# Gated cross-attention block: scores as stacked 96-row contractions, projections one section earlier, mask as pairs of 64-row matmuls

## The chip, the cores and the metric

One core of one Trainium2 chip runs the whole kernel. The metric is the device time of one execution in microseconds (us), as the median of several runs. The profile shows one further execution, with its own time.

## The reference

The input x has 128 sequences of 128 tokens of width 256; ctx has the same shape. Per sequence:

```python
x = x + tanh(g_xattn) * mha(layernorm(x), ctx, ctx)   # 16 heads of 16, causal, biases on q, k, v, o
x = x + tanh(g_ffn) * bitlinear(silu(bitlinear(n, w_gate)) * bitlinear(n, w_up), w_down)   # n = layernorm(x)
```

The attention is softmax(q k / 4) v with a causal mask. A bitlinear rounds each activation row to 8 bits by the row's maximum and the weight matrix to three values by its mean magnitude; the inner width is 1024. All inputs and outputs are float32.

## The kernel before

A tile is one sequence: 128 tokens on the partitions. Two sequences are a pair, and there are 64 pairs. Setup loads and transposes the weights, splits the attention weights into a high and a low part (F32R), rounds the feed-forward weights, and fills constants. The main part is written out in full by Python loops: a section belongs to one tile, `s` is 0 for even tiles and 1 for odd ones, and each engine's `body(c)` lists its work in a section. Every engine runs its list in order, and semaphores connect the engines.

The work is staged. In the section of tile t the kernel does the attention of tile t, the output projection of t-1, the gate and up matmuls of t-2 and the down projection of t-3, and it projects for the next pair: K in an even section (`s` = 0), Q and V in an odd one. Products of F32R operands take three terms, high x high, low x high and high x low (`TERMS`).

The scores of a half (eight heads, two PSUM banks, S_B[half]) are six matmuls of 512 columns (L507). The keys stand in `k_blk` block-diagonally for four heads at a time: 64 rows hold the four heads, and the other 64 rows hold pieces of the causal mask, with matching selection rows in `q_t`. SP makes `k_blk` by eight DMAs a pair out of `k_t` (L473), in the odd section. Q's high part is cast on ACT (`q_high`, L757), its low part made on DVE (`q_low`, L935).

After the scores, DVE takes the row maxima (`top`, L849). For half 0 DVE subtracts the maximum into `prob` (`shift`, L856) and ACT takes exp of it (L711). For half 1 ACT takes exp with the maximum as its bias in eight instructions (L717). PE transposes the probabilities (L515), ACT copies them to `prob_t` (L724), and PE multiplies them with the values (L526); a column of ones gives the row sums. ACT copies the result to `o_raw`, PE transposes it back (L533), DVE divides (L862, L865), PE transposes again (L539), ACT and DVE split it (L736, L880), and PE projects it (L549). PE's wait list for that is

```python
pe.wait_ge(ot_hi, c.tile(1))
pe.wait_ge(ot_lo, c.tile(1))
wait(pe, y_ok, c.tile(3))
```

where `y_ok` counts the results y (`result`, L944): the down projection and the output projection share a bank. Then DVE adds the residual (`residual`, L888), takes the norm's statistics (L891, L895), and POOL centres and rounds the rows.

The feed-forward has gate and up matmuls per half (L607) into one bank each, tanh on ACT (L732), and two instructions per half on DVE (`gated`, L872 and L876). Half 1's matmuls wait for half 0's h, since they write over the same banks. `row_scales` (L904 to L913) and `hidden_scales` (L919 to L929) find the rounding factors, POOL rounds h (L1064), PE transposes it (L614), ACT copies it to `h_t` (L768), and PE projects it down (L624).

On DVE the even section's order is: out_natural, top 0, norm_stats, shift, top 1, out_t, result, gated 0, first_norm, residual, gated 1, row_scales, hidden_scales. The odd section's is: top 0, shift, out_natural, top 1, out_t, result, residual, gated 0, row_scales, q_low, gated 1, hidden_scales. Many waits are followed by an increment of a semaphore `held` that nothing waits for (`hold`).

## Time and profile before

| | |
|---|---|
| median of 3 runs | 1930.83 us (1930.03 to 1931.12) |
| the profiled execution: time | 1932.1 us |
| the profiled execution: span, first to last instruction | 1930.4 us |
| busy: PE | 1747.9 us (91%) |
| busy: DVE | 1658.1 us (86%) |
| busy: ACT | 1434.1 us (74%) |
| busy: POOL | 1053.1 us (55%) |
| DMA queue of SP | 88.13 MB, 22.4% of 16 engines |
| mean granted clock of TensorE | 0.990 |

PE, DVE, ACT and POOL are the engines; PEld is PE's weight load. Busy time is the time in which an engine executes anything, and matmuls overlap each other. L507 is line 507 of the kernel before. In a timeline, the bracket at the end gives the idle time of the engine just before the instruction and what ended it.

### The profile page before, as it was taken

How to read it: one execution, taken by the hardware profiler on the slowest of the kernel's cores; microseconds unless marked ns; L12 is line 12 of the kernel's file. 1: busy time of each engine (PE TensorE's matmuls, PEld its weight loads, DVE VectorE, ACT ScalarE, POOL GpSimd, SP SyncE). 2: the span in 40 equal slices, each digit the busy share in tenths (PEclk: the TensorE clock that was granted, in tenths of full speed). 3: DMA queues.
4: the chain of work that ended last, by engine and by line, in shares of the span. 5: the costliest groups of instructions: out<-in, count | busy, mean ns of one | idle time of the engine just before them, and what ended most of it. 6: DMA issues, size and time to landing. Idle time of an engine off the chain costs nothing. (4 is left out here: it accounts for less than half of the span.)

```text
span 1930.4 us, 46249 instructions
## 1 busy us (share of the span) xinstructions
PE 1747.9 (91%) x15430; PEld 1396.7 (72%) x15430; DVE 1658.1 (86%) x3609; ACT 1434.1 (74%) x2897; POOL 1053.1 (55%) x1623
## 2 busy tenths in 40 slices
PE   3799999999999999999999999999999999999984
PEld 2677777777777777777777777777777777777762
DVE  4588988988988888888898898898898898898884
ACT  3577777787777787777777777777777777778772
POOL 4455555556556556555555555555555555655641
PEclk9999999999999999999999999999999999999996
DMA  3222122122122122122122222222212212212210
GB/s 106 45 53 44 43 53 46 42 55 49 37 56 48 37 57 48 38 55 48 40 52 48 43 50 50 44 47 53 42 46 53 43 45 53 50 38 56 48 20 11
DMA packets 131900, 91.22 MB, mean 47 GB/s; under 512 B 13521, under 2 KB 131409, under 8 KB 131665
## 3 DMA queue, kind: packets, MB, share of 16 engines
q1 hardware_dynamic: 130416, 88.13, 22.4%
q8 instruction: 126, 2.06, 0.4%
q14 instruction: 110, 0.89, 0.2%
q10 hardware_dynamic: 1248, 0.14, 0.1%
HBM read 37.88 MB, written 16.78 MB: 28 GB/s over the span
## 5 line engine op out<-in xcount | busy, mean ns | idle before, releaser
L507 PE MATMUL psum<-k_blk,q_t 128*128 128x512 f32 x1536 | 419.1, 408 | 1.2 <-DVE q_t L935 1.2
L1041 POOL TENSOR_SCALAR xc<-x,ln 128x256 f32<-128x256 f32 x128 | 61.3, 479 | 485.5 <-DVE ln L898 485.5
L849 DVE TENSOR_REDUCE row_max<-psum 128x8 f32<-128x1024 f32 x256 | 311.2, 1215 | 7.1 <-PE psum L507 6.9
L507 PEld LDWEIGHTS psum<-k_blk,q_t 128*128 128x128 f32 x1536 | 268.8, 188 | 62.1 <-issue 14.1
L717 ACT ACTIVATE prob<-psum,row_max 128x128 f32<-128x128 f32 x1024 | 277.4, 385 | 12.7 <-DVE row_max L849 12.6
L1064 POOL TENSOR_SCALAR hq<-h,sm 128x1024 f16<-128x1024 f32 x128 | 143.2, 1119 | 226.6 <-DVE sm L929 220.5
L724 ACT COPY prob_t<-psum 128x1024 f32<-128x1024 f32 x256 | 262.4, 1025 | 5.1 <-PE psum L515 1.4
L515 PE MATMUL psum<-ident,prob 128*128 128x128 f32 x2048 | 255.1, 273 | 4.4 <-ACT prob L711 3.9
L515 PEld LDWEIGHTS psum<-ident,prob 128*128 128x128 f32 x2048 | 228.8, 141 | 6.6 <-ACT prob L711 5.1
L732 ACT ACTIVATE th<-psum,sm 128x512 f32<-128x512 f32 x256 | 178.8, 698 | 14.9 <-PE psum L607 13.2
L872 DVE SCALAR_TENSOR_TENSOR gu<-th,psum 128x512 f32<-128x512 f32 x256 | 174.9, 683 | 10.9 <-ACT th L732 6.8
L876 DVE TENSOR_TENSOR h<-gu,psum 128x512 f32<-128x512 f32 x256 | 175.9, 687 | 8.8
L773 ACT COPY o_raw<-psum 128x512 f32<-128x512 f32 x128 | 75.1, 587 | 139.4 <-PE psum L526 139.4
L607 PE MATMUL psum<-wg_t,xq_t 128*128 128x512 f16 x512 | 155.0, 385 | 21.7 <-DVE h L876 20.5
L526 PE MATMUL psum<-prob_t,v_sb 128*32 128x128 f32 x4096 | 151.6, 277 | 19.0 <-ACT prob_t L724 19.0
L768 ACT ACTIVATE h_t<-psum 128x1024 f16<-128x1024 f16 x128 | 131.0, 1023 | 41.0 <-PE psum L614 39.6
L856 DVE TENSOR_TENSOR prob<-psum,row_max 128x1024 f32<-128x1024 f32 x128 | 155.6, 1216 | 2.2
L919 DVE TENSOR_REDUCE sm<-h 128x1 f32<-128x1024 f32 x128 | 155.5, 1215 | 2.2
L711 ACT ACTIVATE prob<-prob 128x1024 f32<-128x1024 f32 x128 | 139.2, 1087 | 20.9 <-DVE prob L856 20.9
L607 PE MATMUL psum<-wu_t,xq_t 128*128 128x512 f16 x512 | 153.7, 382 | 0.0
L624 PE MATMUL psum<-wd_t,h_t 128*128 128x256 f16 x1024 | 135.9, 277 | 18.3 <-ACT h_t L768 18.3
L526 PEld LDWEIGHTS psum<-prob_t,v_sb 128*32 128x32 f32 x4096 | 100.2, 109 | 68.3 <-ACT prob_t L724 35.5
(116 smaller groups left out, 3729.9 us busy)
## 6 DMA issues: line engine op xcount, KB each, us to landing
k_blk<-k_t SPq DMA_DIRECT2D x512, 64.0 KB, 2.4
c_in<-in_ctx SPq DMA_DIRECT2D x64, 256.0 KB
x_in<-in_x SPq DMA_DIRECT2D x64, 256.0 KB
out<-y SPq DMA_DIRECT2D x128, 128.0 KB
g_nat<-in_L_ffn_w_gate SPq DMA_DIRECT2D x1, 1024.0 KB, 10.5
g_nat<-in_L_ffn_w_up SPq DMA_DIRECT2D x1, 1024.0 KB, 12.8
g_nat<-in_L_ffn_w_down SPq DMA_DIRECT2D x1, 1024.0 KB, 14.4
w_nat<-in_L_xattn_Wq SPq DMA_DIRECT2D x1, 256.0 KB, 4.1
```

What stands on the lines that cost most here:

```text
L507: last = nc.tensor.matmul(dst, q_t[:, b, a, half, c.s, :], k_blk[:, w, half, c.s, 4 * b:4 * b + 4, :], start=n == 0, stop=n == len(TERMS) - 1)
L515: last = nc.tensor.transpose(S_B[half][:, n * P:(n + 1) * P], prob[:, HPC * half + n, :], ident[:, :])
L526: last = nc.tensor.matmul(B6[VW * j:VW * (j + 1), g * P:(g + 1) * P], v_sb[:, c.s, n, :], prob_t[:, n, :], start=True, stop=True)
L607: last = nc.tensor.matmul(dst, xq_t[:, ic, :], w[:, ic, half * HALF:(half + 1) * HALF], start=ic == 0, stop=ic == DC - 1)
L717: last = nc.scalar.activation(prob[:, HPC + n, :], S_B[1][:, n * P:(n + 1) * P], ACT.Exp, bias=row_max[:, HPC + n:HPC + n + 1])
L724: nc.scalar.copy(prob_t[:, HPC * half:HPC * (half + 1), :].rearrange("p h k -> p (h k)"), S_B[half]).then_inc(p_ok[half], 1)
L732: nc.scalar.activation(th[:, half, :], GATE, ACT.Tanh, scale=row(sm, c.s, G_FACTOR)).then_inc(th_ok[half], 1)
L849: nc.vector.tensor_reduce(out=row_max[:, HPC * half:HPC * (half + 1)], in_=S_B[half].rearrange("p (h k) -> p h k", k=P), axis=AX.X, op=ALU ...
L856: nc.vector.tensor_tensor(prob[:, 0:HPC, :], S_B[0].rearrange("p (h k) -> p h k", k=P), row_max[:, 0:HPC].unsqueeze(2).to_broadcast((P, HP ...
L872: nc.vector.scalar_tensor_tensor(out=gu[:, half, :], in0=th[:, half, :], scalar=1.0, in1=UP, op0=ALU.add, op1=ALU.mult).then_inc(gu_ok[hal ...
L876: nc.vector.tensor_tensor(h[:, half, :], gu[:, half, :], GATE, ALU.mult).then_inc(h_ok[half], 1)
L919: nc.vector.tensor_reduce(out=row(sm, t, H_MAX), in_=h[:, :, :].rearrange("p a b -> p (a b)"), axis=AX.X, op=ALU.max, apply_absolute_value ...
```

## The change

- Scores: Q and K get a stacked form. `q_stk` holds 96 rows, high, low and high part of two heads; `k_stk` holds high, high and low part, block-diagonally for the two heads. One matmul with 96 rows then adds the three terms for two heads (256 columns); a half has four of them. Both are double-buffered and filled by DMA: six copies for K (`spread_k`, even section) and three for Q (`spread_q`, odd section). The rows of Wq, Wk and their biases are loaded in another order so that the copies are plain.
- Mask: constants `late_q` and `causal` in BF16. A half gets four matmuls of 256 columns on 64 rows each; each two in a row use different rows and different banks. They come before the waits for K and Q.
- Projections: K for the pair after next is projected in the odd section, Q and V for the next pair in the even one: each one section earlier. v_sb gets two buffers; the bias-added residual `xb` gets three, and its copy `x_res` goes.
- Softmax: both halves are shifted first (half 1 on ACT with Identity in place of Exp), transposed as shifted scores, and exp is taken as they are moved out of PSUM to `prob_t`.
- Q's split moves to POOL (`split_qk`); `q_high` and `q_low` go.
- Both sections get one order on every engine, near that of the odd section before. `norm_stats` and `first_norm` run in the odd section only, `add_bias` in the even one.
- The increments of `held` go. Setup's tiles are freed before the main part.

```diff
+Q_STACK, K_STACK = (HI, LO, HI), (HI, HI, LO)
...
+    PAIR_HD = 2 * HD
+    STACK = len(TERMS) * PAIR_HD
+    HB = HEADS // (2 * DC)
...
+        late_q = sb("late_q", [P, 2, 2, KB], BF16)
+        causal = sb("causal", [P, 2, KB], BF16)
...
+        xb = sb("xb", [P, 3, 2, D])
...
+        q_stk = [sb(f"q_stk{n}", [STACK, HB, DC, 2, P], F32R) for n in range(2)]
+        k_stk = [sb(f"k_stk{n}", [STACK, 2, HB, DC, 2, P], F32R) for n in range(2)]
+        v_sb = sb("v_sb", [P, 2, 2, HEADS, VW])
...
+                self.proj = i + 1 + s
+                self.projects = 0 <= self.proj < PAIRS
+                self.more = 0 <= self.proj and self.proj + 1 < PAIRS
+                self.spread = 0 <= i + 1 < PAIRS
+                self.norm = s == 1 and 0 <= i + 2 < PAIRS
...
+                self.ahead = 0 <= t + 1 < N_SEQ
...
-                    for g in range(HPC):
-                        rows = slice(HD * g, HD * (g + 1))
-                        sp.dma_start(k_blk[rows, :, :, :, g, :].rearrange("p a c s k -> p (a c s) k").bitcast(F32),
-                                     k_t[rows, :, :, :, :].rearrange("p a c s k -> p (a c s) k").bitcast(F32)).then_inc(kb_ld, 16)
+                    p = c.even // 2 + 1
+                    sp.wait_ge(k_hi, 2 * p + 2)
+                    sp.wait_ge(k_lo, 2 * p + 2)
+                    wait(sp, s_mm[1], 2 * p - 2)
+                    for n, part in enumerate(K_STACK):
+                        for a in range(2):
+                            at = n * PAIR_HD + a * HD
+                            sp.dma_start(k_stk[p % 2][at:at + HD, a].rearrange("e h c s k -> e h (c s k)").bitcast(F32),
+                                         k_t[64 * a:64 * a + 64, part].rearrange("p c s k -> p (c s k)").bitcast(F32)
+                                         ).then_inc(k_ld, 16)
+
+                def spread_q(c):
+                    p = c.even // 2 + 1
+                    sp.wait_ge(q_hi, 2 * p + 2)
+                    sp.wait_ge(q_lo, 2 * p + 2)
+                    wait(sp, s_mm[1], 2 * p - 2)
+                    for n, part in enumerate(Q_STACK):
+                        sp.dma_start(q_stk[p % 2][n * PAIR_HD:(n + 1) * PAIR_HD].rearrange("e h c s q -> e h (c s q)").bitcast(F32),
+                                     q_t[:, part].rearrange("p c s q -> p (c s q)").bitcast(F32)).then_inc(q_ld, 16)
...
                 def body(c):
-                    if c.s == 0 and c.more:
+                    if c.spread:
+                        if c.s == 0:
+                            spread_k(c)
+                        else:
+                            spread_q(c)
+                    if c.s == 1 and c.more:
...
-                def scores(c, half):
-                    pe.wait_ge(q_hi, c.even + (c.ahead + 2))
-                    pe.wait_ge(q_lo, c.even + (c.ahead + 2))
-                    pe.wait_ge(kb_ld, c.even * (8 * HPC) + (8 * HPC) * (c.ahead + 2))
-                    wait(pe, p_ok[half], c.tile(1))
-                    for b in range(2):
-                        dst = S_B[half][:, b * BANK:(b + 1) * BANK]
-                        for n, (a, w) in enumerate(TERMS):
-                            last = nc.tensor.matmul(dst, q_t[:, b, a, half, c.s, :],
-                                                    k_blk[:, w, half, c.s, 4 * b:4 * b + 4, :],
-                                                    start=n == 0, stop=n == len(TERMS) - 1)
+                def scores(t, half):
+                    p, s = t // 2, t % 2
+                    wait(pe, p_ok[half], t)
+                    for j in range(2):
+                        for b in range(2):
+                            rows = slice(KB * b, KB * (b + 1))
+                            dst = S_B[half][:, b * BANK:(b + 1) * BANK].rearrange("p (h k) -> p h k", k=P)
+                            nc.tensor.matmul(dst[:, :, KB * j:KB * (j + 1)],
+                                             late_q[rows, j, :, :].rearrange("p a b -> p (a b)"),
+                                             causal[rows, j, :].unsqueeze(1).to_broadcast((KB, 4, KB)),
+                                             start=j == 0, stop=False, skip_group_check=True)
+                    pe.wait_ge(k_ld, 6 * 16 * (p + 1))
+                    pe.wait_ge(q_ld, 3 * 16 * (p + 1))
+                    for g in range(4):
+                        h, c = (4 * half + g) // DC, g % DC
+                        last = nc.tensor.matmul(S_B[half][:, 2 * g * P:(2 * g + 2) * P], q_stk[p % 2][:, h, c, s, :],
+                                                k_stk[p % 2][:, :, h, c, s, :],
+                                                start=False, stop=g % 2 == 1, skip_group_check=True)
                     last.then_inc(s_mm[half], 1)
...
-                def probs_t(c, half):
-                    pe.wait_ge(s_exp[half], c.tile(0))
+                def shifted_t(c, half):
+                    pe.wait_ge(s_sub[half], c.tile(0))
                     for n in range(HPC):
-                        last = nc.tensor.transpose(S_B[half][:, n * P:(n + 1) * P], prob[:, HPC * half + n, :], ident[:, :])
+                        last = nc.tensor.transpose(S_B[half][:, n * P:(n + 1) * P], s_low[:, HPC * half + n, :], ident[:, :])
                     last.then_inc(p_tr[half], 1)
...
+                    pe.wait_ge(x1_ok, min(c.tile(2), N_SEQ))
+                    if c.s == 1 and c.spread:
+                        pe.wait_ge(v_ok, c.even + 4)
...
+                    if c.ffn:
+                        quant_t(c)
+                    if c.attn:
+                        scores(c.t, 1)
+                    if c.projects:
+                        inputs_t(c)
+                    if c.outp:
+                        out_natural(c)
+                    if c.down:
+                        hidden_t(c)
+                    if c.outp:
+                        out_t(c)
+                    if c.down:
+                        down(c)
+                    if c.ffn:
+                        gate_up(c, 0)
+                    if c.outp:
+                        out_proj(c)
+                    if c.projects:
+                        project_qk(c)
+                    if c.attn:
+                        shifted_t(c, 0)
+                        shifted_t(c, 1)
+                    if c.ffn:
+                        gate_up(c, 1)
+                    if c.projects and c.s == 0:
+                        project_v(c)
+                    if c.ahead:
+                        scores(c.t + 1, 0)
+                    if c.attn:
+                        values(c, 0)
+                        values(c, 1)
...
-                def exp(c, half):
-                    if half == 0:
-
-                        act.wait_ge(s_sub, c.tile(0))
-                        v = prob[:, 0:HPC, :]
-                        nc.scalar.activation(v, v, ACT.Exp).then_inc(s_exp[0], 1)
-                        return
-
+                def shift(c):
                     act.wait_ge(s_max[1], c.tile(0))
                     wait(act, p_tr[1], c.tile(1))
                     for n in range(HPC):
-                        last = nc.scalar.activation(prob[:, HPC + n, :], S_B[1][:, n * P:(n + 1) * P], ACT.Exp,
+                        last = nc.scalar.activation(s_low[:, HPC + n, :], S_B[1][:, n * P:(n + 1) * P], ACT.Identity,
                                                     bias=row_max[:, HPC + n:HPC + n + 1])
-                    last.then_inc(s_exp[1], 1)
-
-                def probs_out(c, half):
+                    last.then_inc(s_sub[1], 1)
+
+                def exp(c, half):
                     act.wait_ge(p_tr[half], c.tile(0))
                     wait(act, pv_mm[half], c.tile(1))
-                    nc.scalar.copy(prob_t[:, HPC * half:HPC * (half + 1), :].rearrange("p h k -> p (h k)"),
-                                   S_B[half]).then_inc(p_ok[half], 1)
+                    nc.scalar.activation(prob_t[:, HPC * half:HPC * (half + 1), :].rearrange("p h k -> p (h k)"),
+                                         S_B[half], ACT.Exp).then_inc(p_ok[half], 1)
...
+                    if c.ffn:
+                        quant_t(c)
+                    if c.projects:
+                        inputs_t(c)
+                    if c.down:
+                        hidden_t(c)
+                    if c.outp:
+                        out_t(c)
+                    if c.attn:
+                        shift(c)
+                    if c.ffn:
+                        tanh(c, 0)
+                    if c.projects:
+                        project_qk(c)
+                    if c.attn:
+                        exp(c, 0)
+                    if c.ffn:
+                        tanh(c, 1)
+                    if c.attn:
+                        exp(c, 1)
+                    if c.projects and c.s == 0:
+                        project_v(c)
+                    if c.attn:
+                        values(c)
...
-                def q_low(c):
-                    dve.wait_ge(q_hi, c.pair(0))
-                    for b, rows in enumerate(halves):
-                        nc.vector.tensor_tensor(q_t[rows, b, LO].rearrange("p c s q -> p (c s q)"), q_f[rows, :],
-                                                q_t[rows, b, HI].rearrange("p c s q -> p (c s q)").bitcast(F32),
-                                                ALU.subtract).then_inc(q_lo, 1)
-
...
+                    if c.attn:
+                        top(c, 0)
+                        shift(c)
+                    if c.outp:
+                        out_natural(c)
+                    if c.attn:
+                        top(c, 1)
+                    if c.norm:
+                        norm_stats(c)
+                    if c.outp:
+                        out_t(c)
+                    if c.down:
+                        result(c)
+                    if c.outp:
+                        residual(c)
+                    if c.ffn:
+                        gated(c, 0)
+                    if c.norm:
+                        first_norm(c)
+                    if c.outp:
+                        row_scales(c)
+                    if c.ffn:
+                        gated(c, 1)
+                        hidden_scales(c)
...
+                def split_qk(c):
+                    if c.s == 1:
+                        pool.wait_ge(k_cp, c.pair(0))
+                        wait(pool, k_ld, 6 * 16 * c.proj)
+                        whole, dst, hi_ok, lo_ok = k_f, k_t, k_hi, k_lo
+                    else:
+                        pool.wait_ge(q_cp, c.pair(0))
+                        wait(pool, q_ld, 3 * 16 * c.proj)
+                        whole, dst, hi_ok, lo_ok = q_f, q_t, q_hi, q_lo
+                    split(whole[:, :], [dst[:, n].rearrange("p c s q -> p (c s q)") for n in (HI, LO)], hi_ok, lo_ok, c)
...
+                    if c.projects:
+                        split_inputs(c)
+                    if c.outp:
+                        centre(c)
+                    if c.norm:
+                        first_norm(c)
+                    if c.projects and c.s == 0:
+                        add_bias(c)
+                    if c.outp:
+                        quantise(c)
+                    if c.ffn:
+                        quantise_hidden(c)
+                    if c.projects:
+                        split_qk(c)
```

## Rows read from the trace of the kernel before

**Rows 1.** Windows: busy us (x instructions) of each engine, PEclk, DMA share, GB/s.

```profile
600.00:628.70 28.70, 26.89 (x240) 21.58 (x240) 25.54 (x56) 22.15 (x46) 16.24 (x25) 1.00 0.23 47
...
1877.30:1891.40 14.10, 9.93 (x94) 6.76 (x92) 11.55 (x25) 8.44 (x17) 3.43 (x7) 1.00 0.04 12
```

**Rows 2.** Timeline of DVE, tiles 38 and 39: start us, us, engine, line, idle before.

```profile
600.37 1.21 DVE L849 TENSOR_REDUCE row_max<-psum 128x8 f32<-128x1024 f32 x1
601.50 0.74 DVE L951 BATCH_NORM_STATS2 st<-x_in 128x6 f32<-128x256 f32 x2
602.17 1.21 DVE L856 TENSOR_TENSOR prob<-psum,row_max 128x1024 f32<-128x1024 f32 x1
...
612.92 1.22 DVE L849 TENSOR_REDUCE row_max<-psum 128x8 f32<-128x1024 f32 x1
...
617.87 0.48 DVE L944 SCALAR_TENSOR_TENSOR y<-psum,sm,x 128x256 f32<-128x256 f32 x1 [0.39 <-PE psum L624]
619.48 0.42 DVE L888 TENSOR_TENSOR x<-psum,x_res 128x256 f32<-128x256 f32 x1 [1.13 <-PE psum L549]
...
623.35 1.68 DVE L935 TENSOR_TENSOR q_t<-q_f,q_t 64x512 fp32r<-64x512 f32 x2
625.05 0.69 DVE L872 SCALAR_TENSOR_TENSOR gu<-th,psum 128x512 f32<-128x512 f32 x1
...
629.07 1.21 DVE L849 TENSOR_REDUCE row_max<-psum 128x8 f32<-128x1024 f32 x1
```

**Rows 3.** Timeline of DVE, the section of tile 127.

```profile
1877.29 1.21 DVE L849 TENSOR_REDUCE row_max<-psum 128x8 f32<-128x1024 f32 x1
...
1881.79 0.48 DVE L944 SCALAR_TENSOR_TENSOR y<-psum,sm,x 128x256 f32<-128x256 f32 x1
1883.40 0.42 DVE L888 TENSOR_TENSOR x<-psum,x_res 128x256 f32<-128x256 f32 x1 [1.13 <-PE psum L549]
...
1884.46 0.18 DVE L895 BATCH_NORM_AGGREGATE mv<-st 128x2 f32<-128x6 f32 x1 [0.17 <-DVE st L891]
...
1885.52 0.69 DVE L876 TENSOR_TENSOR h<-gu,psum 128x512 f32<-128x512 f32 x1
...
1888.06 0.69 DVE L872 SCALAR_TENSOR_TENSOR gu<-th,psum 128x512 f32<-128x512 f32 x1 [0.72 <-ACT th L732]
...
1891.40 0.25 DVE L862 RECIPROCAL row_rcp<-psum 128x16 f32<-128x16 f32 x1
```

**Rows 4.** Timeline of PE: three rows of a pair, three of tile 127's section.

```profile
618.50 0.94 PE L549 MATMUL psum<-w_t,o_t 128*128 128x256 f32 x6
619.28 1.58 PE L579 MATMUL psum<-xn_t,w_t 128*128 128x256 f32 x12
...
622.44 0.59 PE L607 MATMUL psum<-wg_t,xq_t 128*128 128x512 f16 x2
...
1880.44 0.44 PE L539 MATMUL psum<-ident,o_n 128*128 128x128 f32 x2 [1.04 <-DVE o_n L865]
...
1882.42 0.94 PE L549 MATMUL psum<-w_t,o_t 128*128 128x256 f32 x6
...
1886.27 0.60 PE L607 MATMUL psum<-wg_t,xq_t 128*128 128x512 f16 x2
```

**Rows 5.** Windows of line 507 alone, one pair: PE busy, PEld busy.

```profile
600.00:628.70 28.70, 6.55 (x24) 4.20 (x24) 1.00 0.23 47
```

**Rows 6.** Group of instructions on ACT, whole run: busy us, mean ns, idle before.

```profile
L711 ACT ACTIVATE prob<-prob 128x1024 f32<-128x1024 f32 x128 | 139.2, 1087 | 20.9 <-DVE prob L856 20.9
```

**Rows 7.** Timeline of POOL: the second split of an odd section.

```profile
616.67 0.62 POOL L1074 TENSOR_SCALAR xn_t<-x_f 128x512 fp32r<-128x512 f32 x1
617.44 1.27 POOL L1076 TENSOR_TENSOR xn_t<-x_f,xn_t 128x512 fp32r<-128x512 f32 x1 [0.15 <-POOL xn_t L1074]
```

**Rows 8.** SP's DMA issues, and the DMA window that follows.

```profile
616.86 5.80 SPq L473 DMA_DIRECT2D k_blk<-k_t  x8
...
618.00:624.00 6.00, 6.00 (x48) 5.25 (x46) 4.47 (x13) 5.90 (x13) 3.39 (x6) 1.00 0.67 88
```

More of the change, by code:

```diff
@@ new lines, in _ @@
+                nc.gpsimd.tensor_copy(causal[:, 0, :], past[:, 0, :])
+                put(past[:, 1, :], past[:, 0, :], ALU.not_equal, MASKED, 1 - KB, 0).then_inc(masks, 1)
+                pool.wait_ge(masks, 4)
+                put(late_q[:, 1, 1, :], same[:, 0, :], ALU.not_equal, 0.0, 1 - P, 0)
+                put(causal[:, 1, :], past[:, 1, :], ALU.not_equal, MASKED, 1 - P, 0)
+                for n in range(2):
+                    nc.gpsimd.memset(k_stk[n][:, :, :, :, :, :].bitcast(F32), 0.0)
@@ L744, in project_qk @@
                 def project_qk(c):
[L745 removed]
+                    read, dst, bias, free, done = (k_mm, k_f, bk_c, k_lo, k_cp) if c.s == 1 else (q_mm, q_f, bq_c, q_lo, q_cp)
                     act.wait_ge(read, c.pair(0))
@@ L847, in top @@
                     dve.wait_ge(s_mm[half], c.tile(0))
-                    wait(dve, s_exp[1] if half == 1 else s_sub, c.tile(1))
+                    wait(dve, s_sub[half], c.tile(1))
                     nc.vector.tensor_reduce(out=row_max[:, HPC * half:HPC * (half + 1)],
```

469 lines of the change are left out of this document (109 added, 360 removed).

## The prediction

> **What bounds the kernel now.** I began with the busy time per stretch [rows 1]. In one pair of tiles, 28.70 us, PE is busy 26.89, DVE 25.54, ACT 22.15 and POOL 16.24. No engine has a large reserve, so a share of busy time does not say what the change is worth. The section in the row below it, the last one with attention (tile 127), projects nothing: PE is busy only 9.93 of 14.10 us there, at full clock.
>
> Next the order of time on DVE, over one pair [rows 2]. The score maximum of half 0 (L849) starts at 600.37 (even section), 612.92 (odd) and 629.07: the sections last 12.55 and 16.15 us. DVE runs its list in order and hardly stops. In the odd section it waits 0.39 us for the down projection (L944) and 1.13 for the output projection (L888), and it carries the low half of Q (L935), 1.68 us, between the row scales and the second gated half.
>
> Last, the section of tile 127 on DVE and PE [rows 3, 4]. It uses the odd section's order, which the change gives to both sections, and has no projection and no L935. It is the nearest thing to the new section that the trace shows. It still lasts 1891.40 - 1877.29 = 14.11 us, and DVE waits 1.13 and 0.72 us in it. So its length is a loop through several engines. With D the start of the first maximum: output transpose on PE at D+3.15, once DVE has made o_n; output projection at 5.13; residual on DVE at 6.11; first half of h done at 8.92 (1885.52 + 0.69); second gate and up on PE at 8.98; second gated half on DVE, behind tanh on ACT, at 10.77; next section at 14.11. PE stands idle within it, yet the loop does not close sooner.
>
> **The change on PE.** The 24 score matmuls of a pair, busy 6.55 us [rows 5], go. In come 16 of 256 columns with 96 rows, and 16 bf16 ones of 256 columns on 64 rows. The nearest row is the output projection, six of 256 columns in 0.94 us, 0.157 each [rows 4]. The first 16 come to 2.5 us. The masks cost 1.25 if the two of a pair run side by side and 2.5 if they don't. I take 1.5, nearer the low end, because the two use different rows and banks. PE saves about 2.5 us a pair, between 1.5 and 2.8. The trace has no pair of 64-row matmuls and no switch into that form. At worst, switching eats all the saving, and PE costs what it costs now. The Trainium skill (TensorEngine Tiling (Array Packing), Key Properties) says that changing the tiling mode drains TensorE; no row here shows such a drain, and by the page part of the saving would be lost. The saving itself lies off the loop. The second half's scores stand early in the section, and PE waits later in it at the output transpose, for o_n.
>
> **ACT and POOL.** ACT loses the separate exp (L711, 1.09 us a tile [rows 6]), Q's high cast and the copies of the residual. The exp now replaces a copy of the same 1024 elements out of PSUM, and the eight shifts with a bias replace eight exps of the same shape; I cost both exchanges at nothing. Tanh of the second half starts when gate and up are ready, and the exp in front of it depends only on transposes that PE does before them. POOL gains one split a pair. Every section now has two splits in a row, as the odd one has now: the second starts at 616.67 and ends at 617.44 + 1.27 = 618.71 [rows 7], D+5.79. The projection behind it is due on PE at 5.13 + 0.78 (618.50 to 619.28 [rows 4]) = D+5.91. That leaves 0.1 us, so a little more delay would show.
>
> **DVE.** The increments of the semaphore held go; one of them stands in front of bn_aggr (L895), where DVE idles 0.17 us [rows 3]. At most that is won ahead of the second gate, and PE reaches that gate later anyway, as shown below: nothing. L935 goes, 1.68 us a pair. It stood over the wait for the second tanh. From the start of the projection to the second gate is 622.44 - 619.28 = 3.16 us on PE [rows 4]; from there to the gated half is 1888.06 - 1886.27 = 1.79. In the present odd section that half could start at 624.23, against 625.05 now [rows 2]. So removing 1.68 us of work would win only 0.8 even with nothing else changed.
>
> *New even section* (projects Q and V, no norm): the loop of 14.11, but PE, now with a projection ahead of the transposes, reaches the second gate at 5.91 + 3.16 = 9.07 instead of 8.98, so 14.20 us. V's projection, 12 matmuls of at most 0.157 or 1.9 us, stands behind that gate; PE, with 26.89 - 2.5 = 24.4 us of work in a pair of 29, has room for it ahead of the next section.
>
> *New odd section* (projects K, norm for a later pair): the norm statistics stand ahead of the low half of o and of the result. They move DVE by 602.17 - 601.50 = 0.67 us [rows 2]. At first sight they fill the wait of 1.13. But PE's output projection waits for the low half and for y. In tile 127's section y starts at 1881.79 and takes 0.48, and the projection follows at 1882.42, 0.15 us later [rows 3, 4]: nothing between them is free. So out_proj moves from 5.13 to 5.80, and everything behind it moves too. 14.20 + 0.67 = 14.87 us. The remaining norm instructions (bn_aggr and two small ones) fall into the wait of 0.72.
>
> The pair thus takes 29.07 against 28.70, 0.37 us more. Over 62 pairs in which the pipeline is full that is +22.9 us. Near the end there are no norms: tile 125 saves 0.67, and tile 126 takes 14.11 instead of 12.55, +1.56; together +0.9. The start has one more section on paper, but the chain K, norm, Q is the same there and the DMA of Q replaces that of K; I take 0, and put 3 us either way in the range. Sum +23.8. The profiled execution has a span of 1930.4 and took 1932.1, so it would become 1955.9; the median of the runs is 1.3 lower, which gives 1954.6.
>
> **DMA and SP.** A pair spreads 8 copies of 64 KB now, 512 KB, and 6 of 128 and 3 of 256 KB after, 1536 KB. SP takes 5.80 us to issue eight [rows 8], 0.73 each; the copies run at 88 GB/s in that stretch, with the DMA engines busy 0.67 [rows 8]. K has more than a section of time. Q is tight: its split ends at D+3.75 of the odd section (where the second split starts now), the three issues end near D+5.9, and scores need it near D+10.8. At 88 GB/s, 786 kB take 8.9 us, and Q would land near D+13.8. If the copies go at the pace of the issues (256 KB per 0.73 us), it is there by about D+7. I take a middle, in time: the old packets had 512 bytes, the new ones 2 KB, and the old rate is just that of 64 KB per issue. On SP, storing y and loading x stand behind the K copies. They are issued about D+8 to D+9; y's buffer is wanted two sections later and x in the next, so it costs nothing.
>
> **Rivals.**
> *Work removed is time removed.* DVE keeps its waits and loses 1.68: the pair takes 27.02, total 1930.8 - 104 = 1827. It decides from the point where the residual finds the output projection done (D+5.0) and the second tanh comes before the row scales end. For it: DVE is busy 89% and PE 94% [rows 1]. Against: tile 127's section, with PE 70% busy, still has both waits. The Trainium skill (Perfetto Trace Analysis, Identifying the Most-Contended Engine) says to optimise the engine with the highest occupancy first; by it the relief of DVE and PE would pay, and the row of tile 127 disagrees.
> *The norm statistics hide in the wait.* Both sections take 14.20: 28.40 a pair, total 1930.8 - 18.6 + 0.9 = 1913. It needs a projection that doesn't wait for y; its only support is the 1.13 us gap.
> *PE or Q's data late.* With Q at D+13.8, scores, two value blocks, and the next section's transposes push the hidden transpose, and with it h_t and the down projection, to about 0.5 us past D+3.4: +31 us, 1985. A score block as dear as now would, after V's projection, do about the same.
>
> **From these to numbers.** Forecast 0.52 (its own range 1940 to 1970), work removed 0.12, norm hidden 0.13, late PE or data 0.15, and 0.08 in between or beyond, mostly near 1930. 0.2% is 3.9 us, about what a measurement can tell from no change. Faster 0.26, same 0.08, slower 0.66. The range leaves out the first rival and the far ends: 1908 to 1990.
>
> **What would show it.** In the profile after: maxima of half 0 alternately 14.2 and 14.9 us apart; DVE waits near 1.1 us at the residual in both, and 0.4 to 0.8 at the second gated half behind tanh; PE busy under 88% with waits at the output transpose; ACT under 20 us a pair; score matmuls waiting for no DMA. I am wrong if the two waits vanish, or if PE waits for q_stk or its clock falls: PE at 70% kept its clock in tile 127's section [rows 1], but not for 1800 us.

## The result, and the profile after

The changed kernel takes 1962.69 us (median of 4 runs, 1960.31 to 1964.41) beside 1930.74 for the kernel before on the same chip: ratio 1.0165, 95% interval 1.0147 to 1.0183. It is slower, as forecast; the forecast was 1954.6. Its profiled execution has a span of 1960.4 us, 30.0 more than before.

The page of the profile after, its line of busy us, share of the span and instructions, and that of Q's copies (KB each, median us from issue to landing):

```profile
PE 1632.6 (83%) x15942; PEld 1290.6 (66%) x15942; DVE 1557.0 (79%) x3481; ACT 1203.0 (61%) x2505; POOL 1129.2 (58%) x1756
...
q_stk<-q_t SPq DMA_DIRECT2D x192, 256.0 KB, 5.7
```

PE is 115 us less busy than before, DVE 101, ACT 231, and the kernel is slower. The windows of one pair and of tile 127's section answer to [rows 1]:

```profile
600.00:629.02 29.02, 24.99 (x250) 19.84 (x250) 23.95 (x55) 18.64 (x39) 17.45 (x28) 1.00 0.52 83
1904.86:1920.33 15.47, 9.95 (x86) 6.73 (x86) 11.63 (x25) 7.77 (x16) 3.43 (x7) 0.89 0.03 9
```

The timeline of DVE after, an odd and an even section, answers to [rows 2, 3]:

```profile
599.46 1.22 DVE L759 TENSOR_REDUCE row_max<-psum 128x8 f32<-128x1024 f32 x1
...
603.60 0.74 DVE L853 BATCH_NORM_STATS2 st<-x_in 128x6 f32<-128x256 f32 x2
...
604.59 0.47 DVE L846 SCALAR_TENSOR_TENSOR y<-psum,sm,x 128x256 f32<-128x256 f32 x1
606.20 0.42 DVE L798 TENSOR_TENSOR x<-psum,xb 128x256 f32<-128x256 f32 x1 [1.14 <-PE psum L542]
...
610.94 0.69 DVE L782 SCALAR_TENSOR_TENSOR gu<-th,psum 128x512 f32<-128x512 f32 x1 [0.63 <-ACT th L684]
...
614.27 1.21 DVE L759 TENSOR_REDUCE row_max<-psum 128x8 f32<-128x1024 f32 x1
...
618.78 0.48 DVE L846 SCALAR_TENSOR_TENSOR y<-psum,sm,x 128x256 f32<-128x256 f32 x1
620.39 0.42 DVE L798 TENSOR_TENSOR x<-psum,xb 128x256 f32<-128x256 f32 x1 [1.13 <-PE psum L542]
...
622.37 0.69 DVE L786 TENSOR_TENSOR h<-gu,psum 128x512 f32<-128x512 f32 x1
...
625.14 0.69 DVE L782 SCALAR_TENSOR_TENSOR gu<-th,psum 128x512 f32<-128x512 f32 x1 [1.06 <-ACT th L684]
...
628.48 1.22 DVE L759 TENSOR_REDUCE row_max<-psum 128x8 f32<-128x1024 f32 x1
```

The maxima are 14.81 us (odd) and 14.21 us (even) apart, where 14.87 and 14.20 were forecast, and both waits of the loop stand in both sections. The timeline of PE after, the same pair, answers to [rows 4]:

```profile
605.21 0.95 PE L542 MATMUL psum<-w_t,o_t 128*128 128x256 f32 x6 [0.42 <-DVE y L846]
...
610.12 0.39 PE L492 MATMUL psum<-causal,late_q 64*128 64x256 bf16 x4
611.48 0.71 PE L500 MATMUL psum<-k_stk,q_stk 96*128 96x256 f32 x4 [0.96 <-DMA q_stk<-q_t]
...
613.35 0.39 PE L492 MATMUL psum<-causal,late_q 64*128 64x256 bf16 x4
613.67 0.74 PE L500 MATMUL psum<-k_stk,q_stk 96*128 96x256 f32 x4
614.28 0.63 PE L559 MATMUL psum<-ident,xn 128*128 128x128 f32 x4
...
615.63 0.62 PE L607 MATMUL psum<-ident,hq 128*128 128x128 f16 x8 [0.29 <-POOL hq L935]
617.43 0.44 PE L532 MATMUL psum<-ident,o_n 128*128 128x128 f32 x2 [1.18 <-DVE o_n L775]
...
619.41 0.95 PE L542 MATMUL psum<-w_t,o_t 128*128 128x256 f32 x6
620.19 1.58 PE L572 MATMUL psum<-xn_t,w_t 128*128 128x256 f32 x12
...
623.36 0.59 PE L600 MATMUL psum<-wg_t,xq_t 128*128 128x512 f16 x2
```

In the odd section the output projection does wait for y, 0.42 us. PE waits 0.96 us for Q's copies there, which the forecast did not have; what that cost, the experiments say. Across the span of the profile: the maximum of tile 2 starts at 91.48 us instead of 83.88 (+7.60); the 62 pairs from there take 1799.40 instead of 1780.85 (+18.55), at a granted clock of 1.00 in both; tile 126's section takes 13.98 instead of 12.56 (+1.42); what follows the start of tile 127's maximum takes 55.5 instead of 53.1 (+2.4). Of these 2.4, 1.4 are tile 127's own section: 15.47 us where it was 14.11, at a granted clock of 0.89 where it was 1.00. PE there:

```profile
1906.21 0.62 PE L607 MATMUL psum<-ident,hq 128*128 128x128 f16 x8 [1.43 <-POOL hq L935]
1908.02 0.69 PE L532 MATMUL psum<-ident,o_n 128*128 128x128 f32 x2 [1.18 <-DVE o_n L775]
1908.50 1.91 PE L616 MATMUL psum<-wd_t,h_t 128*128 128x256 f16 x8
```

Behind two waits of 1.43 and 1.18 us the down projection takes 1.91 us; within the pairs it takes 1.04.

### The profile page after: what moved, and what is told of

Its sections match the earlier page's. It is cut to its first block, busy times and chain, and to the rows that moved or that the text cites. A ratio compares the mean times of both kernels' runs of the same rounds, so it can differ in the third digit from the quotient of the medians.

```text
span 1960.4 us, 46062 instructions
## 1 busy us (share of the span) xinstructions
PE 1632.6 (83%) x15942; PEld 1290.6 (66%) x15942; DVE 1557.0 (79%) x3481; ACT 1203.0 (61%) x2505; POOL 1129.2 (58%) x1756
## 4 chain that ended last, share of the span: by engine, by line
DVE 39%; PE 39%; issue 13%; ACT 5%; POOL 2%; DVEq 0%; DMA 0%; POOLq 0%; SPq 0%; ACTq 0%
PE psum L508 11%; DVE row_max L759 11%; PE psum L572 9%; PE psum L600 8%; DVE sm L828 8%; PE psum L542 5%; DVE gu L782 4%; DVE h L786 4%; ACT th L684 4%; PE psum L616 3%; DVE st L853 2%; DVE row_rcp L772 2%; DVE o_n L775 1%; DVE sm L833 1%; PE psum L532 1%
## 5 line engine op out<-in xcount | busy, mean ns | idle before, releaser
L935 POOL TENSOR_SCALAR hq<-h,sm 128x1024 f16<-128x1024 f32 x128 | 143.2, 1119 | 337.9 <-DVE sm L838 337.9
L669 ACT ACTIVATE s_low<-psum,row_max 128x128 f32<-128x128 f32 x1024 | 278.7, 384 | 33.6 <-DVE row_max L759 33.6
L676 ACT ACTIVATE prob_t<-psum 128x1024 f32<-128x1024 f32 x256 | 261.7, 1023 | 5.7 <-PE psum L508 1.7
L508 PE MATMUL psum<-ident,s_low 128*128 128x128 f32 x2048 | 245.1, 273 | 0.0
L500 PE MATMUL psum<-k_stk,q_stk 96*128 96x256 f32 x1024 | 188.6, 306 | 62.8 <-DMA q_stk<-q_t 62.8
L508 PEld LDWEIGHTS psum<-ident,s_low 128*128 128x128 f32 x2048 | 227.5, 141 | 0.0
L500 PEld LDWEIGHTS psum<-k_stk,q_stk 96*128 96x128 f32 x1024 | 137.8, 189 | 119.5 <-issue 106.9
L532 PE MATMUL psum<-ident,o_n 128*128 128x128 f32 x256 | 56.5, 303 | 149.8 <-DVE o_n L775 149.8
L766 DVE TENSOR_TENSOR s_low<-psum,row_max 128x1024 f32<-128x1024 f32 x128 | 156.7, 1224 | 4.4
L542 PEld LDWEIGHTS psum<-w_t,o_t 128*128 128x128 f32 x768 | 99.8, 190 | 74.4 <-issue 73.4
L542 PE MATMUL psum<-w_t,o_t 128*128 128x256 f32 x768 | 122.4, 295 | 27.8 <-DVE y L846 25.8
```

Of the source, the lines that this page charges most:

```text
L500: last = nc.tensor.matmul(S_B[half][:, 2 * g * P:(2 * g + 2) * P], q_stk[p % 2][:, h, c, s, :], k_stk[p % 2][:, :, h, c, s, :], start=Fals ...
L508: last = nc.tensor.transpose(S_B[half][:, n * P:(n + 1) * P], s_low[:, HPC * half + n, :], ident[:, :])
L542: last = nc.tensor.matmul(XO_PS, o_t[:, a, ic, :], w_t[3][:, w, ic, :], start=n == 0, stop=n == 3 * DC - 1)
L669: last = nc.scalar.activation(s_low[:, HPC + n, :], S_B[1][:, n * P:(n + 1) * P], ACT.Identity, bias=row_max[:, HPC + n:HPC + n + 1])
L676: nc.scalar.activation(prob_t[:, HPC * half:HPC * (half + 1), :].rearrange("p h k -> p (h k)"), S_B[half], ACT.Exp).then_inc(p_ok[half], 1)
```

## The experiments

Theory: the section is a loop through DVE, PE and ACT, closed by the order in which each engine does its work; work taken off beside it wins nothing. Rival: PE's work or Q's data set the section. Each run has the kernel before beside it on the same chip; ratios are to that, and since the runs were on several chips, two experiments are best compared by their ratios. "Long" sections are those above 15.2 us between two shifts on DVE, in the profiled execution, among the 62 even ones from tile 2 on; the expectations recorded below have slightly other counts of them.

**norm_late: the norm statistics behind the result.**

```diff
-                    if c.norm:
-                        norm_stats(c)
                     if c.outp:
                         out_t(c)
                     if c.down:
                         result(c)
+                    if c.norm:
+                        norm_stats(c)
```

> In the changed kernel DVE makes the norm statistics behind the result instead of ahead of o's low half. Theory 1 (the section is a loop through DVE, PE and ACT, and the output projection waits for y): in odd sections the output projection starts 0.6 to 0.67 us earlier and the statistics fill DVE's wait of 1.14 us before the residual, so the odd section falls from 14.81 to about 14.2 us; over 61 pairs that is -37 to -41 us, 1962.7 to about 1923. Rival (the pair is set by the amount of work on an engine or by Q's data, for which PE waits 0.9 us in odd sections): nothing changes, 1963 within 4 us.

Measured: 1949.11 us, ratio 1.0089 (1.0059 to 1.0119). The odd section is 14.19, the 0.6 us are won. But 20 of the 62 even sections are long, 15.4 to 16.1, and of the some 37 us that the theory expected, 14 are left. PE in such a stretch of norm_late:

```profile
608.07 0.71 PE L500 MATMUL psum<-k_stk,q_stk 96*128 96x256 f32 x4 [1.57 <-DMA q_stk<-q_t]
...
610.93 1.22 PE L500 MATMUL psum<-k_stk,q_stk 96*128 96x256 f32 x4
```

and the windows around it (the column before the last two is the granted clock):

```profile
606.50:608.10 1.60, 0.03 (x1) 0.06 (x1) 1.14 (x2) 1.31 (x2) 1.41 (x4) 1.00 1.11 194
608.10:612.70 4.60, 4.60 (x50) 3.48 (x51) 4.37 (x7) 0.87 (x2) 2.50 (x6) 0.63 0.06 18
```

The wait for q_stk has grown from 0.96 to 1.57 us; right behind it TensorE's clock falls to its lower level, 1.2 GHz (granted clock 0.63 over the 4.6 us): the same four scores that take 0.74 us take 1.22. The loop has lost a term, and a second limit that it had hidden comes out.

**onat_early and even_old: two other orders.** even_old, whose edit is too long to show, gives even sections an order near that of the even sections before. onat_early is norm_late with DVE's out_natural between the first maximum and the shift:

```diff
                     if c.attn:
                         top(c, 0)
-                        shift(c)
                     if c.outp:
                         out_natural(c)
+                    if c.attn:
+                        shift(c)
```

> norm_late, and DVE also divides the attention output (out_natural) between the first maximum and the shift instead of behind the shift. Theory 1: o_n is ready about 1.2 us earlier, at D+1.9; the down projection then starts when h_t is ready, near D+3.05 instead of 3.42, so each section loses about 0.35 us, 45 us over 128 sections, to about 1880. If the attention output is late on PE (transposed back at D+1.1 to 1.5) DVE may wait a little. Rival (work on DVE bounds): the order of the same instructions changes nothing against norm_late.

> The changed kernel, with the even section in an order near that of the kernel before: gate and up of half 0 ahead of the down projection, tanh of half 0 ahead of the shift of half 1, the first gated half ahead of the residual, the second gate ahead of the projections. Theory 1 (one order for both sections is what costs, since it leaves the waits of 1.13 and 1.06 us on DVE in the even section): the even section falls from 14.21 to about 12.7 us; PE then ends it late, and the odd section may take up to 0.9 us more; the pair takes 27.3 to 28.2 us against 29.02, total 1855 to 1912. Rival (the order makes no difference, the new data path costs): 1963 within 4 us.

Measured: onat_early 1955.06 (1.0128), all sections but two 14.4 in place of 14.2: DVE now waits 0.29 to 0.35 us for PE's transpose of o_raw, and what this puts off is the second maximum (at 3.27 us of the section, where the changed kernel has it at 3.01). The mean clock is 0.983, the changed kernel's 0.981. even_old 1963.29 (1.0168): 13.25 in even sections and 15.31 in odd ones, a pair of 28.56 where undisturbed, and 20 even sections of 14.5 to 15.2 after falls of the clock. Neither total is where the theory put it (1880 and 1855 to 1912); that of even_old is even the rival's 1963, but the rival had no change in the sections, and they changed by 0.95 and 0.5 us. The section's length follows the order on the engines in each of these, as the theory says; the amount of PE's work is the same in all.

**before_noqlow: the kernel before without its 1.68 us of L935.** It leaves out the low part of Q in the scores.

> The kernel before without the low half of Q: DVE does not compute it, and its place in the scores holds zeros (low x high is left out of the scores). Theory 1 (L935 stands over the wait for the second tanh): the odd section loses 0.8 us, -50 us, to about 1881. Rival (work removed is time removed): 1.68 us a pair, -104 to -107 us, to about 1825. A second rival (PE, busy 94 per cent, is the bound already): less than 20 us.

Measured: 1920.15 us, ratio 0.9943 (0.9929 to 0.9958), 10.9 us faster, 0.19 a pair. DVE in its odd section:

```profile
622.09 0.69 DVE L873 SCALAR_TENSOR_TENSOR gu<-th,psum 128x512 f32<-128x512 f32 x1 [1.42 <-ACT th L733]
```

Of the 1.68 us, 1.42 are now a wait for tanh. The time alone would fit the expectation's second rival (PE is the bound, under 20 us). But PE had ended the second gate and up by 620.72, and tanh starts at 621.37. ACT stands in the way, with Q's cast and a copy ahead of that tanh and no idle time between:

```profile
619.04 1.26 ACT L758 CAST q_t<-q_f 64x512 fp32r<-64x512 f32 x2
620.33 1.01 ACT L725 COPY prob_t<-psum 128x1024 f32<-128x1024 f32 x1
621.37 0.69 ACT L733 ACTIVATE th<-psum,sm 128x512 f32<-128x512 f32 x1
```

**mask_twice: more work for PE in the changed kernel.**

```diff
-                    for j in range(2):
+                    for j in (0, 1, 1, 1):
```

> One edit on the changed kernel: the second mask matmul pair of each half is issued three times instead of once, so each score block has eight mask matmuls instead of four (the masked entries get three times the mask, which changes no other value). Four mask matmuls took 0.32 us, so TensorE works 1.3 us more in a pair, 83 us over the kernel, about half of what the change took off it. Theory (TensorE's work is off the path that sets the sections; this is why taking it off won nothing): sections stay at 14.2 and 14.8, time within 5 us of 1962.7. Rival (TensorE's own work sets the sections): +0.65 us a section, 2046. Rival 2 (half is hidden behind the waits for o_n of 1.18 us, the other half isn't): 2000.

Measured: 1961.92 us, the changed kernel's own time. PE busy time in each 100 us rises from some 86.4 to 88.8 us, which is 0.7 us a pair and not the 1.3 expected (eight masks take 0.54 us start to start, four 0.32); the sections stay at 14.19 and 14.81, the wait for q_stk shrinks from 0.96 to 0.75. More load on PE is free here. That less would be free too, no run shows by itself.

**split_early, norm_split, three: Q's copies earlier.**

```diff
+                    if c.projects and c.s == 0:
+                        split_qk(c)
                     if c.ffn:
                         quantise_hidden(c)
-                    if c.projects:
+                    if c.projects and c.s == 1:
                         split_qk(c)
```

> One edit on the changed kernel: in an even section GpSimd splits Q into its two parts before it quantises the hidden row, in the 3.17 us in which it waits for the hidden scale, instead of after it. Q's copies can then leave about 3.5 to 4.5 us earlier and land before TensorE asks. Theory (the order on VectorE and ScalarE sets the sections, Q's data are hidden as the kernel stands): the 0.96 us wait of the scores for q_stk in the odd section goes, the sections stay at 14.2 and 14.8, and the time stays within 4 us of the changed kernel: 1959 to 1965. Rival (Q's data set the odd section, which is the longer one): the odd section falls by up to 0.6 us, to 14.2, and the time by up to 37 us, to 1926.

> Both edits on the changed kernel: the norm statistics after the result on VectorE (norm_late) and Q's split ahead of the hidden quantisation on GpSimd (split_early). norm_late alone gave 1949 instead of the some 1922 that its 14.18 and 14.20 us sections would give, since some 25 even sections of 62 ran 15.4 to 16.1 us behind a TensorE that had waited for Q's copies and then had half its clock. Theory (Q's copies are the second limit, and the wait for them is what the clock falls on): no wait for q_stk, the granted clock stays at 1.0 in the loop, all sections 14.2, and the time is 1919 to 1928. Rival 1 (the clock falls for another reason, the wait is beside it): the long even sections stay, 1945 to 1955. Rival 2 (the extra DMA traffic slows other loads): between, 1930 to 1945, with waits for x_in or the stores.

> norm_split with the even section in the order near that of the kernel before (even_old). even_old ran 13.25 and 15.31 us undisturbed, with norm statistics costing some 0.67 of the 15.31, and had some 20 even sections of 14.6 to 15.3 after a fall of TensorE's clock. Theory: even section 13.25, odd 14.6, no falls of the clock, pair 27.9, so 62 times 1.17 below the changed kernel's 29.02: 1886 to 1896. Rival (the odd section is late for the tanh and TensorE, not for the statistics): odd stays at 15.3, pair 28.55, 1930 to 1940. Rival 2: with TensorE's work closer together the wait for Q comes back in spite of the earlier split, and the clock falls in the even sections: 1905 to 1925.

Measured: split_early 1992.25 (ratio 1.0301, 1.0253 to 1.0349; the profiled execution, at 1999.95, is the slowest of its four), norm_split 1981.85 (1.0246, 1.0226 to 1.0266), three 1980.17 (1.0235). No expectation had these times; norm_split's first rival, that the clock falls for another reason than the wait, had the right reading at 1945 to 1955. The wait for q_stk is gone in all of them, as meant, and all of them are slower than with it. The undisturbed sections are what they were (14.2 and 14.8; 14.2 and 14.2), but split_early has 22 long even sections, norm_split 36. three (norm_split with the order of even_old) has 13.25 and 15.25, and 37 even sections of 14.3 to 15.2: the statistics hardly shorten its odd section, as its first rival had it (at 28.5 us a pair where undisturbed; the time, 1980, is the falls'). My reading of norm_late, that the clock falls only because of the wait for Q's copies, goes with this: here it drops with no such wait at all. PE in norm_split around a long section:

```profile
616.70 0.60 PE L526 MATMUL psum<-ident,o_raw 128*128 128x128 f32 x4
618.26 0.62 PE L607 MATMUL psum<-ident,hq 128*128 128x128 f16 x8 [0.96 <-POOL hq L935]
620.05 0.44 PE L532 MATMUL psum<-ident,o_n 128*128 128x128 f32 x2 [1.17 <-DVE o_n L775]
620.32 1.47 PE L616 MATMUL psum<-wd_t,h_t 128*128 128x256 f16 x8
...
622.94 1.63 PE L542 MATMUL psum<-w_t,o_t 128*128 128x256 f32 x6
```

and its windows:

```profile
618.00:620.30 2.30, 0.87 (x10) 0.70 (x11) 2.23 (x5) 1.02 (x1) 2.06 (x4) 1.00 0.00 0
620.30:624.40 4.10, 4.10 (x20) 2.84 (x19) 1.64 (x3) 3.23 (x10) 2.12 (x3) 0.58 0.56 104
```

PE had 0.96 us more slack. The loop is no shorter, so the slack moved on to the next thing PE waits for: hq. The changed kernel has 0.29 and 1.18 us of waits there and keeps its clock; here it is 0.96 and 1.17, close together, and the clock is low right behind them (0.58), just where down, gate and out_proj are on the loop. So the standing still itself seems to matter, and where it falls, not what it waits for. It is not the whole cause: the same two waits stand in the 25 other even sections of norm_split, which stay short. In split_early they stand in 61 even sections, and the long ones are those of tiles 6, 8 and 10 and all nineteen from 50 to 86. What decides between them stays open. The reading makes a new prediction: give PE useless work there.

**norm_split_fill, norm_fill, fill_both: useless transposes.** Nothing reads their result. Here the six ahead of the wait for o_n, which all three have; fill_both has six more in even sections, ahead of the wait for hq.

```diff
                 def out_t(c):
+                    if c.down:
+                        pe.wait_ge(x1_ok, min(c.tile(2), N_SEQ))
+                        if c.s == 1 and c.spread:
+                            pe.wait_ge(v_ok, c.even + 4)
+                        for _ in range(6):
+                            nc.tensor.transpose(DOWN[:, 0:P], ident[:, :], ident[:, :])
                     pe.wait_ge(on_ok, c.tile(1))
```

> norm_split, and TensorE makes six transposes of the identity into the bank of the down projection (nothing reads them) just before it waits for o_n, where it stood for 1.17 us in every section. split_early and norm_split had no wait for Q's copies and yet half the clock for some 3 us in 21 and 33 even sections: it fell behind the waits of 0.96 us for the hidden row and 1.17 us for o_n, 0.6 us of transposes between them; the changed kernel has 0.29 and 1.18 there and keeps its clock. So the first theory (the wait for Q's copies makes it fall) is given up. [...] Rival 1 (the falls come from the load or the temperature, more work makes them worse): 1980 to 2000. Rival 2 (the transposes push TensorE's own chain, o_t and down): sections of 14.4 to 14.6, 1935 to 1950.

> norm_late (Q's copies late, waits of 1.5 to 1.9 us for q_stk at the scores of the odd section) with the same six useless transposes before the wait for o_n. In norm_late the clock fell right behind the wait for q_stk, which the transposes don't fill. Theory: the falls stay for that wait, about as many long even sections as in norm_late, 1940 to 1955. Rival (the standing still before o_n belongs to the fall too): no falls, 1919 to 1930.

> norm_split_fill, and in even sections six more useless transposes before TensorE waits for the hidden row, where it still stood for 0.96 us. TensorE's busy time rises by another 0.75 us a pair (norm_split_fill: 93% busy). Theory (the order on VectorE sets the sections, TensorE's load doesn't, and its clock stays up as long as it has little standing still in a stretch): sections stay at 14.2, the clock at 1.0, time 1916 to 1924, and it repeats that this order is below the kernel before. Rival (near 94% TensorE becomes the bound, or the transposes delay the hidden row's): even sections of 14.4 or more, 1930 or more.

If the standing still ahead of o_n brings the clock down, norm_split_fill should keep a clock of 1.0 and take 1919 to 1930 us.

Measured: norm_split_fill 1921.31 us, ratio 0.9945 (0.9932 to 0.9959): some 58 us less than norm_split by the ratios, by nothing but work that nobody needs. No section is long, the clock is 1.00 all through the loop. (One of its five runs stands apart at 2016.02 us, with a mean granted clock of 0.843 where the others have 0.983 to 0.987; its cause stays open, and with it whether the filling always holds.) norm_fill 1957.61 (1.0137), 29 long even sections: the clock also falls behind the wait for Q's copies, in each of these cases behind one of 1.5 us or more, and transposes elsewhere don't help it. So the early split and the filling are both needed. That the same transposes at another place of norm_split would not do as well, no run shows. fill_both 1917.30 us (1916.62 to 1918.14, five runs), ratio 0.9923 (0.9909 to 0.9937). PE in fill_both, the same place:

```profile
602.01 0.82 PE L614 MATMUL psum<-ident 128*128 128x128 f32 x6
603.14 0.62 PE L617 MATMUL psum<-ident,hq 128*128 128x128 f16 x8 [0.31 <-POOL hq L945]
603.60 0.82 PE L535 MATMUL psum<-ident 128*128 128x128 f32 x6
604.94 0.44 PE L538 MATMUL psum<-ident,o_n 128*128 128x128 f32 x2 [0.51 <-DVE o_n L785]
```

The Trainium skill (TensorE: Matmul & The Clock Gate, HAM oscillation — how this bites in real kernels) tells of a loop in which waits for DMA bring the clock down again and again. norm_late and norm_fill agree; norm_split shows the same (0.58 in the window above) with waits for POOL and DVE, and DMA share 0.00 in the window before it.

**no_first_copy: what the start consists of.**

```diff
                     p = c.even // 2 + 1
+                    if p == 0:
+                        return
```

> The changed kernel without the nine copies of K and Q of the first pair: the stacked operands of pair 0 are zeros, so its two tiles see only the mask in place of their scores. It shows what of the 7.60 us by which the maximum of tile 2 comes later than before (91.48 against 83.88 us) is Q's copies, whose landing the first scores wait for at 64.42. Theory 1 (what sets the start is TensorE's order: the projections of pair 1 stand before the scores of tiles 0 and 1 and wait for GpSimd's halves, at 58.35 and 71.03): the first maximum comes 2 to 3 us earlier, but that of tile 1 at 77 to 79 and that of tile 2 at 90 to 92 as now, the time 1959 to 1964. Theory 2 (the copies set the start): the maximum of tile 2 at 84 to 86, the time 1955 to 1957.

Measured: 1958.14 us. The maximum of tile 2 starts at 88.70: 2.78 of the 7.60 us go with the first copies, more than theory 1 allowed and well short of theory 2. Not all of the 2.78 is waiting for data. The maximum of tile 1 starts only 1.24 us earlier (77.38 instead of 78.62); behind it the projection of 12 matmuls takes 1.58 us instead of 2.76 and the 16 transposes 1.91 instead of 2.16, since the clock that is 0.51 from 85 to 88 us in the changed kernel is 1.00 there. The other 4.8 are not the copies. PE's timeline and two windows of the changed kernel's start, and below them the first of the two in the kernel before, show what is there:

```profile
58.35 2.90 PE L572 MATMUL psum<-c_t,w_t 128*128 128x256 f32 x12 [3.05 <-POOL c_t L946]
...
64.42 1.05 PE L500 MATMUL psum<-k_stk,q_stk 96*128 96x256 f32 x4 [2.84 <-DMA q_stk<-q_t]
...
71.03 2.90 PE L572 MATMUL psum<-xn_t,w_t 128*128 128x256 f32 x12 [3.01 <-POOL xn_t L946]
```

```profile
64.00:70.00 6.00, 3.60 (x16) 2.59 (x16) 3.58 (x3) 1.43 (x5) 1.31 (x3) 0.55 0.78 124
70.00:75.00 5.00, 3.98 (x19) 4.01 (x20) 0.00 (x0) 2.17 (x8) 2.30 (x4) 0.52 0.41 77
...
64.00:70.00 6.00, 6.00 (x66) 5.01 (x64) 1.92 (x2) 4.77 (x12) 3.40 (x5) 1.00 0.01 1
```

The projections of pair 1 now stand on PE ahead of the first transposes and wait 3.05 and 3.01 us for POOL's halves, and the clock is near half (0.55 and 0.52), where it was 1.00 in the kernel before from 64 to 70 us. How much of the 4.8 is the one and how much the other was not separated.

## Why the prediction was right, and where its size was off

**The loop: right, almost term by term.** With D = 614.27, the start of the even section: output transpose at D+3.16 (forecast 3.15), output projection 5.14 (5.13), the projection behind it 5.92 (5.91), residual 6.12 (6.11), first half of h done 8.79 (8.92), second gate 9.09 (9.07), second gated half 10.87 (10.77 and the 0.09 of the projection), next section 14.21 (14.20). onat_early, even_old and mask_twice show that it is this order and not PE's load.

**The norm statistics: right.** In the odd section y starts at D+5.13 against 4.51 in the even one and the output projection waits for it; the section is 0.60 longer, forecast 0.67. norm_late takes just that away. The pair became 29.02, beside a mean of 28.72 before. The 62 of them cost 18.55 us where the sum had 22.3 (22.9, less the 0.67 of tile 125, which is in the last of them).

**The cost of L935's removal: right in sign, mis-sized.** "Would win only 0.8" was read from DVE and PE; before_noqlow shows 0.19, because ACT's list, with Q's cast and a copy ahead of the second tanh, closes 0.6 us later. It did not enter the sum, as the new section was built from tile 127's.

**PE: right.** The masks take 0.32 us for four, 0.08 each, the low end (0.078): the two of a pair run side by side, and no drain is to be seen between the 64-row and the 96-row matmuls (613.35, 613.67, 614.28). PE is busy 24.99 us a pair, 1.9 less. It won nothing in the loop, and mask_twice shows that giving 0.7 of it back costs nothing.

**Q's copies: the value taken was wrong.** They were taken to land between D+7 and D+13.8, "in time" for D+10.8. They landed at D+12.0 (611.48 - 599.46): 786 KB in 8.3 us from the first issue at 603.16 (D+3.7), beside c_in. That is the slow end. The forecast put it at D+13.8, but its own figures, a split that ends at D+3.75 and 8.9 us of copying, give D+12.65. PE waited 0.96 us, and that this costs nothing in the changed kernel was not worked out: here the forecast was lucky. split_early, without the wait, has the same 14.2 and 14.8 in its undisturbed sections. In norm_late, where the wait is some 1.6 us, it cost time, and not by the data but by the clock.

**The start: the term of the sum that failed.** "I take 0, 3 us either way" measured 7.60. The step said that the chain K, norm, Q is the same at the start and the DMA of Q replaces that of K. But the first scores wait 2.84 us for Q's copies; with the clock behind them, the first copies come to 2.8 us at tile 2. And a projection moved up by a section is, at the start, a projection ahead of the first softmax in PE's list. The end was taken as unchanged from the last maximum on and cost 2.4, of which 1.4 are the clock in tile 127's section and 1.0 was not followed up.

**The sum.** +7.6 and +2.4, less 3.9 in the pairs and tile 126, are the 6.2 us, but for rounding, by which the span missed; the rest of the 8.1 is the profiled execution, which lay 0.5 us under its median instead of 1.3 over it.

**What would show it.** PE is at 86%, ACT at 18.6 us a pair, and the two waits stand, though the second is 1.06 us in even sections where 0.4 to 0.8 was named. "I am wrong if PE waits for q_stk" came true, and the time was right all the same: as a sign it was too strict. The clock, the other sign, held in all 62 pairs. It did not hold at the start (0.55 and 0.52) nor in tile 127's section (0.89), the very section whose clock of 1.00 before was taken as the support. In the pairs the margin was small: split_early moved 0.96 us of slack from the wait for q_stk to the one for hq, with the same work, and lost some 26 us by the ratios.

## What to carry to other kernels

Follow one loop through all engines' lists, with its offsets, before a share of busy time is believed; a section of the old kernel that lacks the disputed work is the best measure of the new one. Price the first and last sections by themselves when work is moved up: what is hidden in the loop is bare there. And where PE has slack, look at where it gathers: before shortening a wait, ask which wait grows in its place, and try useless matmuls in it, which cost nothing off the loop and won some 58 us here, in all executions but one.

## What the runs showed of the hardware

- TensorE's clock fell behind two waits of 0.96 and 1.17 us with 0.6 us of f16 transposes between, in 36 of the 61 even sections of norm_split that have them and in 22 of 61 in split_early. It fell behind 1.43 and 1.18 us in tile 127's section of the changed kernel. In the profiled executions it made no section of the pairs long behind 0.29 and 1.18 (changed kernel), 0.96 and 0.51, or 0.31 and 0.51 (the filled ones).
- Behind a wait for q_stk of 1.5 us or more it fell in 20 even sections of norm_late and 29 of norm_fill, and not in all: in both kernels some stayed short behind waits of up to 1.8 us, and in onat_early, where the waits are mostly 1.4 us, it fell once, behind one of 1.62.
- Copies within SBUF in packets of 2 KB were hardly faster, if at all, than the old ones of 512 bytes. From 605 to 611 us of the changed kernel, with c_in's load and a store of y among them, the DMA engines moved 123 GB/s and were busy throughout (share 1.07). The 88 GB/s at a share of 0.67 [rows 8] would come to 131 at a full share, an estimate.
